# A decoder layer's stretch behind the head-pair loop: gating on GpSimd, the last two pairs projected in place, one half of the tokens ahead through both norms

## What is computed

```
x = x + attn(layernorm(x))        # a state-space scan
x = x + xattn(ctx, layernorm(x))  # 0.6 * sigmoid(si + sj + b) + 0.4 * layernorm(x)
x = x + moe(layernorm(x))
```

## Time and profile before

| | |
|---|---|
| median of three runs | 445.43 us (443.49 to 446.92) |
| the profiled execution | 447.58 us, span of its core 445.8 us |
| instructions | 8885 |
| PE busy | 414.9 us, 93% |
| DVE busy | 351.1 us, 79% |
| ACT busy | 225.7 us, 51% |
| POOL busy | 223.3 us, 50% |
| mean granted TensorE clock | 0.976 |

### The profile page before, as it was taken

How to read it: one execution, slowest core, us unless ns; L and a number is a source line. 1 busy time by engine, 2 the same in 40 slices (tenths; PEclk the granted TensorE clock), 3 DMA queues, 4 the chain that set the end, 5 groups by cost and what they waited for, 6 DMA issues and landing times.

```text
span 445.8 us, 8885 instructions
## 1 busy us (share of the span) xinstructions
PE 414.9 (93%) x2959; PEld 318.6 (71%) x2959; DVE 351.1 (79%) x604; ACT 225.7 (51%) x408; POOL 223.3 (50%) x238
## 2 busy tenths in 40 slices
PE   2898999999999999999999977998999999999995
PEld 1686767676667676667676556766789889899885
DVE  3787689889889889889889937947886696786775
ACT  5665545455545545545577430146543653554541
POOL 3444344654544664544577540022738558648661
PEclk9999799999999999999999978999899999999999
DMA  6302101221111212112210040011110201200002
GB/s 189 77 1 53 51 8 53 57 56 55 34 28 50 56 56 56 39 23 51 54 34 32 16 137 2 1 43 50 51 48 24 73 26 45 71 0 1 0 0 96
DMA packets 33607, 20.00 MB, mean 45 GB/s; under 512 B 15816, under 2 KB 31488, under 8 KB 33584
## 3 DMA queue, kind: packets, MB, share of 16 engines
q1 hardware_dynamic: 33584, 19.71, 15.7%
HBM read 17.33 MB, written 1.31 MB: 42 GB/s over the span
## 4 chain that ended last, share of the span: by engine, by line
PE 43%; issue 23%; POOL 14%; DVE 12%; ACT 3%; DMA 2%; SPq 1%; POOLq 1%; DVEq 0%; ACTq 0%
PE bank L1107 30%; POOL g L497 9%; PE bank L1131 4%; DVE conv L887 4%; POOL ce L490 3%; DMA w_raw<-in_L_attn_W_in_dram 1%; PE bank L1315 1%; DVE stats L814 1%; DMA ew_raw<-in_L_ffn_Wdown_dram 1%; ACT conv L561 1%; POOL xp L462 1%; PE bank L1475 1%; PE bank L1293 1%; DVE xres L1006 1%; SPq L325 1%
## 5 line engine op out<-in xcount | busy, mean ns | idle before, releaser
L887 DVE SCALAR_TENSOR_TENSOR conv<-bank,taps,conv 128x510 f32<-128x510 f32 (+2 forms) x204 | 151.6, 746 | 28.3 <-ACT conv L561 23.5
L497 POOL TENSOR_TENSOR g<-g,causal 128x512 f32<-128x512 f32 x64 | 81.6, 1294 | 108.1 <-DVE g L971 108.1
L1131 PE MATMUL bank<-uth,parts 128*128 128x512 f32 x272 | 98.6, 413 | 1.5 <-DVE utl L870 1.0
L561 ACT ACTIVATE conv<-bank,tap_b,taps 128x512 f32<-128x512 f32 x68 | 52.9, 779 | 77.2 <-PE bank L1131 76.8
L523 POOL TENSOR_TENSOR ul<-conv,uh 128x512 fp32r<-128x512 f32 x32 | 42.8, 1353 | 46.6 <-ACT uh L770 33.7
L528 POOL TENSOR_TENSOR parts<-conv,parts 128x512 fp32r<-128x512 f32 x30 | 44.2, 1502 | 36.0 <-ACT parts L784 35.9
L1131 PEld LDWEIGHTS bank<-uth,parts 128*128 128x128 f32 x272 | 51.8, 190 | 10.7 <-issue 1.7
L1131 PE MATMUL bank<-utl,parts 128*128 128x512 f32 x136 | 56.9, 418 | 0.0
L1107 PE MATMUL bank<-ewh,parts 128*128 128x256 f32 x256 | 46.2, 279 | 1.2 <-DVE parts L1094 1.2
L1079 DVE CAST uh<-conv 128x512 fp32r<-128x512 f32 x28 | 26.4, 977 | 22.7 <-ACT conv L766 22.4
L1315 PE MATMUL bank<-conv 64*128 64x128 f32 x512 | 43.4, 289 | 0.3 <-DVE conv L887 0.3
(11 more groups left out here) (204 smaller groups left out, 744.0 us busy)
## 6 DMA issues: line engine op xcount, KB each, us to landing
w_raw<-in_L_attn_W_in_dram SPq DMA_DIRECT2D x17, 256.0 KB, 3.2
ecx<-ecum_dram SPq DMA_DIRECT2D x32, 128.0 KB, 2.9
ew_raw<-in_L_ffn_Wup_dram SPq DMA_DIRECT2D x7, 256.0 KB, 2.8
ew_raw<-in_L_ffn_Wgate_dram SPq DMA_DIRECT2D x7, 256.0 KB, 3.1
ew_raw<-in_L_ffn_Wdown_dram SPq DMA_DIRECT2D x7, 256.0 KB, 3.8
xres<-in_x_dram SPq DMA_DIRECT2D x2, 512.0 KB, 4.1
out_dram<-xres SPq DMA_DIRECT2D x4, 256.0 KB, 2.3
yi<-yev SPq DMA_DIRECT2D x60, 16.0 KB, 1.9
```

The lines of the kernel that those rows point to most:

```text
L497: pool.tensor_tensor(g_v, g_v, causal[:].unsqueeze(1).to_broadcast([P, 4, P]), ALU.mult).then_inc(masked, 1)
L561: act.activation(conv[q][:, j, HALF * h:HALF * (h + 1)], bank[u % 2][:], ACT.Identity, bias=tap_b[q][:, j:j + 1], scale=taps[q][:, j, TAPS ...
L887: dve.scalar_tensor_tensor(out=dst[:, :, d:SEQ], in0=src[:, :, 0:SEQ - d], scalar=taps[q][:, j, TAPS - 1 - d:TAPS - d], in1=dst[:, :, d:SE ...
L1131: ins = pe.matmul(bank[u % 2][:], w, x_t, start=(i == 0), stop=(i == 3 * KD - 1))
```

## The change

- **Pairs.** Pairs 12 and 13 are written out as well. z's gate moves to pairs 12 and 13 (its scratch to `xn`), `pairwise` to pair 13, the scaling of `sig` to pair 14. `gate_y` moves from DVE to POOL: channel half 0 in pairs 13 and 14, half 1 in pair 15, there over its first 96 rows (`EARLY`, pairs 9 to 14).
- **Last two pairs.** Their y is not moved into `yi`. SP brings the matching rows of `zT`, `yD` and `woT` to where y lies (`load_late`, 24 DMAs in all). POOL gates pair 15's y in place (`gate_late`), DVE pair 16's, straight from PSUM (`gate_last`), and PE projects each 16 rows (`late_onto_o`). Every token tile has a bank of its own (`o_tile`).
- **Weights.** The loads of experts 0 and 1 go out in pairs 13 and 14; ACT splits expert 0's in pair 15, expert 1's at the end of the last; POOL makes the rests.
- **Norms.** Inverse roots start from ACT's square root with one Newton step. The first half of the tokens goes through both norms before the second half's first statistics. 58 of the matmuls that nothing reads go, 6 short ones come.
- **Expert 0.** Up starts on the first half, in banks 2 to 5. `route` takes the two-way softmax as `0.5 + 0.5 * tanh` of half the difference, and stands between products 1 and 2.
- **Down biases.** The probabilities are turned at expert 6; the biases are the first matmul of each tile's sum in the last `down`, and the `shift` goes into the last accumulation.

The diff, cut to its core and moved left by eight columns:

```diff
-    with eng.Fori(1, PAIRS // 2 - 1) as k:
+    with eng.Fori(1, PAIRS // 2 - 2) as k:
         body(2 * k, k, 0)
         body(2 * k + 1, k, 1)
-    for n in range(PAIRS - 2, PAIRS + 1):
+    for n in range(PAIRS - 4, PAIRS + 1):
         body(n, n // 2, n % 2)
 def last(n, ahead):
...
+def o_tile(t):
+    return bank[t][:, 0:DM]
+def up_bank(e, v):
+    return bank[2 + v] if isinstance(e, int) and e == 0 else bank[v]
...
+    def load_late(p):
+        r = slice(EARLY + 2 * HD * p, EARLY + 2 * HD * (p + 1))
+        for i in range(4):
+            rows_i = slice(32 * i, 32 * i + 2 * HD)
+            for a, src in enumerate((zT, yD)):
+                sp.dma_start(zsp[rows_i, p, a, :].rearrange("p (h t) -> p h t", h=2),
+                             src[r, 1, :].rearrange("p (h i t) -> p i h t", h=2, i=4)[:, i]).then_inc(zsp_in, 16)
+            sp.dma_start(wsp[rows_i, p, :], woT[r, 1, :]).then_inc(zsp_in, 16)
...
+        if n == PAIRS - 3:
+            load_expert(0, 0)
+        if n == PAIRS - 2:
+            sp.wait_ge(pair_read, 3)
+            load_expert(1, 1)
         if n < PAIRS:
             load_cum(n + 1, 1 - q)
-        if n > 1:
+        if 1 < n < PAIRS:
             sp.wait_ge(y_read, n - 1)
-            place_y(n - 1, 1 - q, (0, 1), yev_out[1 - q])
+            place_y(n - 1, 1 - q, yev_out[1 - q])
...
+        if n >= PAIRS - 1:
+            sp.wait_ge(z_gated, 4)
+            sp.wait_ge(y_init, 1)
+            sp.wait_ge(misc_read, 2)
+            load_late(n - PAIRS + 1)
...
+    def gate_y(k, half):
+        for q in range(2):
+            pool.wait_ge(yev_out[q], 64 * (PAIRS // 4 if k == 0 else PAIRS // 2 - 1))
+        r, c = slice(0, P if k == 0 else EARLY), slice(HALF * half, HALF * (half + 1))
+        link(pool.tensor_tensor(yi[r, k, c], yi[r, k, c], yD[r, k, c], ALU.add))
+        pool.tensor_tensor(yi[r, k, c], yi[r, k, c], zT[r, k, c], ALU.mult).then_inc(yz_done, 1)
+    def gate_late():
+        pool.wait_ge(y_read, PAIRS - 1)
+        pool.wait_ge(zsp_in, 24 * 16)
+        link(pool.tensor_tensor(yev[1][:], yev[1][:], zsp[:, 0, 1, :], ALU.add))
+        pool.tensor_tensor(yev[1][:], yev[1][:], zsp[:, 0, 0, :], ALU.mult).then_inc(late_gated[0], 1)
...
     def body(n, k, q):
+        end = isinstance(n, int) and n == PAIRS
+        if end:
+            decay_c_half(n, q, 0)
+            decay_c_half(n, q, 1)
         for u in range(4):
             pool.wait_ge(g_done, 4 * (n - 1) + u + 1)
             g_v = g[u % 2][:].rearrange("p (i k) -> p i k", k=P)
             pool.tensor_tensor(g_v, g_v, causal[:].unsqueeze(1).to_broadcast([P, 4, P]),
                                ALU.mult).then_inc(masked, 1)
-            if isinstance(n, int) and PAIRS - 2 <= n < PAIRS and 1 <= 4 * (n - PAIRS + 2) + u <= 4:
+            if isinstance(n, int) and PAIRS - 4 <= n < PAIRS - 2 and 1 <= 4 * (n - PAIRS + 4) + u <= 4:
                 v = (u - 1) % 4
                 pool.wait_ge(zgate_done, v + 1)
                 pool.tensor_tensor(z_part(v), z_part(v), zgate(v), ALU.mult).then_inc(z_gated, 1)
-            if u == 1:
+            if isinstance(n, int) and n in (PAIRS - 3, PAIRS - 2) and u == 3:
+                pool.wait_ge(z_gated, 4)
+                gate_y(0, n - PAIRS + 3)
+            if isinstance(n, int) and n == PAIRS - 2 and u == 2:
+                pool.wait_ge(sig_done, T)
+                pool.tensor_scalar(sig[:], sig[:], P_SEM / 2, P_SEM / 2, ALU.mult, ALU.add).then_inc(sig_scaled, 1)
+            if isinstance(n, int) and n == PAIRS - 1 and u >= 2:
+                gate_y(1, u - 2)
+            if u == 1 and end:
+                gate_late()
+            if u == 1 and not end:
                 decay_c(n, k, q)
                 if not last(n, 1):
                     at_least(pool, y_done, 4 * (n - 1))
                     prepare(n + 1, 1 - q)
-        if isinstance(n, int) and n == PAIRS:
-            pool.wait_ge(sig_done, T)
-            pool.tensor_scalar(sig[:], sig[:], P_SEM / 2, P_SEM / 2, ALU.mult, ALU.add).then_inc(sig_scaled, 1)
+        if end:
+            for e in range(2):
+                for j in range(3):
+                    rest_weights(e, e, j)
     over_pairs(pool, body)
...
         first_tap(m, km, r, u)
-        if isinstance(n, int) and n == PAIRS - 2:
+        if isinstance(n, int) and n == PAIRS - 4:
             gate_of_z(u)
-        if isinstance(n, int) and n == PAIRS - 1:
+        if isinstance(n, int) and n == PAIRS - 3:
             pairwise(u)
+        if isinstance(n, int) and n == PAIRS - 1 and u:
+            if u == 1:
+                act.wait_ge(ew_in[0], 48)
+            split_weights(0, 0, u - 1)
...
     def last_pair(n):
         decays(n, 0)
+        decays(n, 1)
+        evacuate_y(n - 1, PAIRS // 2 - 1, 1)
         copy_b(n)
-        evacuate_y(n - 1, PAIRS // 2 - 1, 1)
-        decays(n, 1)
-        act.wait_ge(ew_in[0], 48)
-        split_weights(0, 0, 0)
         copy_state(n)
         decays(n, 2)
         decays(n, 3)
-        evacuate_half(0)
-        split_weights(0, 0, 1)
-        split_weights(0, 0, 2)
-        evacuate_half(1)
+        act.preload_act_table(ACT.Sqrt)
+        act.wait_ge(ew_in[1], 48)
+        for j in range(3):
+            split_weights(1, 1, j)
...
     def expert(e, k, q):
         first = isinstance(e, int) and e == 0
+        if isinstance(e, int) and e == NE - 2:
+            for i in range(2):
+                act.wait_ge(prob_turned, i + 1)
+                act.copy(probT[:, HALF * i:HALF * (i + 1)], bank[4 + i][0:NE, :]).then_inc(prob_read, 1)
         act.wait_ge(eb_done, e + 1)
...
+            if first and v == 1:
+                root(slice(4, 8), 4)
             if first and v == 2:
+                copy_logits(0)
+                root(slice(T + 4, 2 * T), 5)
+                normalise(T + 4, range(4, 6), 5)
                 split_turned(6, 6)
                 split_turned(7, 7)
...
+            if first and v == 1:
+                act.wait_ge(pexp_in, 1)
+                act.activation(lg[:], lg[:], ACT.Tanh).then_inc(pexp_done, 1)
...
+    def inverse_roots(s, i, meanwhile=None):
+        dve.wait_ge(mv_done, i)
         dve.tensor_scalar(var[:, s], mv[:, s, 1], EPS, None, ALU.add)
-        dve.wait_ge(root_done, 1)
+        if meanwhile:
+            meanwhile()
+        dve.wait_ge(root_done, i)
         link(dve.reciprocal(rstd[:, s], rstd[:, s]))
...
+    def gate_last(h):
+        dve.wait_ge(y_done, 4 * (PAIRS - 1) + 2 * (h + 1))
+        if h == 0:
+            dve.wait_ge(yev_out[0], 64 * (PAIRS // 2 - 1))
+            dve.wait_ge(zsp_in, 24 * 16)
+        c = slice(P * h, P * (h + 1))
+        dve.tensor_tensor(yev[0][:, c], bank[7][:, c], zsp[:, 1, 1, c], ALU.add).then_inc(y_read, 1)
+        dve.wait_ge(y_read, PAIRS + h)
+        dve.tensor_tensor(yev[0][:, c], yev[0][:, c], zsp[:, 1, 0, c], ALU.mult).then_inc(late_gated[1], 1)
...
-                gate_y(0, 0)
-            if isinstance(n, int) and n == PAIRS:
-                if u == 1:
-                    gate_y(0, 1)
-                    split_router()
-                    rest_weights(0, 0, 0)
+                split_router()
         if isinstance(n, int) and n == PAIRS:
-            gate_y(1, 0)
+            gate_last(0)
...
-    moments(0, range(4), from_projection)
-    gate_y(1, 1)
-    inverse_roots(slice(0, 4))
     dve.wait_ge(sig_scaled, 1)
+    moments(0, range(4), from_projection, mv_done)
+    inverse_roots(slice(0, 4), 2, lambda: gate_last(1))
     second_block(range(4))
-    moments(T, range(4), from_residual)
-    moments(4, range(4, 8), from_projection)
-    inverse_roots(slice(4, 12))
-    normalise(10, range(2, 4))
+    moments(T, range(4), from_residual, mv_done)
+    inverse_roots(slice(T, T + 4), 3)
+    normalise(T + 2, range(2, 4))
+    rest_turned(4, 0)
+    rest_turned(5, 1)
+    moments(4, range(4, 8), from_projection, mv_done)
+    inverse_roots(slice(4, 8), 4)
     second_block(range(4, 8))
-    moments(12, range(4, 8), from_residual)
-    rest_turned(4, 4)
-    rest_turned(5, 5)
-    inverse_roots(slice(12, 16))
-    normalise(14, range(6, 8))
-    rest_weights(0, 0, 1)
+    moments(T + 4, range(4, 8), from_residual, mv_done)
+    inverse_roots(slice(T + 4, 2 * T), 5)
+    normalise(T + 6, range(6, 8))
     rest_turned(6, 6)
     rest_turned(7, 7)
...
-        link(dve.tensor_scalar(bg[:], sel[:], -NEG, NEG, ALU.mult, ALU.add))
+        link(dve.tensor_scalar(sel[:], sel[:], TOPK - 0.5, 0.5, ALU.is_lt, ALU.mult))
         link(dve.tensor_tensor(lg[:], lg[:], sel[:], ALU.mult))
-        link(dve.tensor_tensor(lg[:], lg[:], bg[:], ALU.add))
-        link(dve.tensor_reduce(mx[:], lg[:], AX.X, ALU.max))
-        dve.tensor_tensor(lg[:], lg[:], mx[:].unsqueeze(2).to_broadcast([P, T, NR]), ALU.subtract).then_inc(pexp_in, 1)
+        link(dve.tensor_reduce(mx[:], lg[:], AX.X, ALU.add))
+        dve.scalar_tensor_tensor(out=lg[:], in0=lg[:], scalar=2.0, in1=mx[:].unsqueeze(2).to_broadcast([P, T, NR]),
```

(91 more changed lines are left out.)

193 lines of the change are left out of this document (70 added, 123 removed).

## The result

The changed kernel takes 455.74 us (median of 4 runs, 454.62 to 456.43) against 445.31 for the kernel before (4 runs, 443.49 to 446.92): ratio 1.0215, 95% interval 1.0183 to 1.0247. It is slower by 10.4 us where 6.1 us less were forecast. The profiled execution took 456.43 us, with a span of 454.7.

A forecast was written before the change was run, and what follows sets the result against it. No engine bounds the whole span; 72.0 us between the last pair and expert 0's down product repeat nothing. Terms -10.8 + 3.7 + 1.0 = -6.1 from 445.43 gave 439.3 us; the range was 432 to 446.

The forecast's parts named there:

- Eight bias matmuls move into the last `down`, where nothing covers them: +3.7.: Last expert's down product: the bias matmuls moved there add 3.7 us uncovered.
- -10.8: Work from the last pairs to expert 0's down product: that product begins at 311.9 against 322.70, gaining 10.8 us.
- +1.0: Expert 6: the transposes of the probabilities stand in PE's queue and add 1.0 us.
- The rival for it: Clock falls more often, in up(0), second half and last `down`, as fillers go: together +4.1, 443.4 us; chance 0.15.
- down(0) at 311.9: Start of expert 0's down product, after the up(1) stall on silu 2 behind route: 311.9, against 322.70.
- First half: First half of tokens through projection and both norms: last rest ends at 277.0 against 289.3, gaining 12.3 us.
- ACT's 8.4 us wait: Last pair: ACT stands 8.4 us waiting for expert weights; its disappearance was a sign that the forecast holds.
- Late inputs: `gate_late` on POOL waits for 24 DMAs landing late: slower than before, up to +25 us, 464; chance 0.07.
- the 3 that I had named as a sign: POOL idle before `gate_late` for over 3 us would show the forecast wrong.
- The pairs did not stall: Rival that POOL's new gates and masks stretch and stall the pairs: +4.8 us, 444.1; chance 0.08.
- Second half and route: Second half's norms beside expert 0 end at 290.4; DVE starts `route` at 300.7, which takes 5.4 us, to 306.1.
- Three falls of the clock: Low clock after PE idles, about 1.7 us charged three times: first half's projection, up(0) and up(1).

The follow-up runs named there:

- experiment 2: Changed kernel with its biases as four grouped fp32 matmuls, 16 rows by 512 columns, ahead of the last down product: 446.17 us, ratio 1.0001.
- the kernel before with the tail part: Kernel before with only its expert 0 bias matmuls and their DVE additions replaced by eight 8-row fp32 ones in the last down product: 456.39 us.
- root and route: Changed kernel with f32r 128-row biases and filler, second half's first root ahead of up: 439.92 us; route ahead of DVE's products, no third filler: 439.03; both: 438.69.

## Why the prediction was wrong

*The step that failed: "Eight bias matmuls move into the last `down`, where nothing covers them: +3.7."* The product went from 5.7 to 20.6 us. By the rows: 3.5 for the matmuls (the product of 9.2 us over 128 rows); 2.4 for the eight changes of row count (8 x 0.3); the rest, 9.0, for half clock from the second tile to the end. Eight rows are the cause of the last two; 128 rows with zeros have neither. In the terms of the sum: +3.7 came out as +14.9, -10.8 as -7.4, +1.0 as +1.2. The rival for it, "the 8-row biases in the last `down` one more" fall, was priced at one fall among others, together +4.1. A fall after a group ends, as in experiment 2. With a few rows in every tile it does not: 19 us at half clock in a product that would have taken 9.

*What I overlooked stood in my own rows.* Of 315.46 to 322.70, clock 0.76, right behind the bias group of the kernel before, I said in the sum only that up(1) "ran partly at low clock too", and charged low clock there for idle PE alone, though PE was busy for all 7.2 us. The rival did tie the fall to the old bias block (with "0.5 to 0.75", where the row has 0.76): the row had been read, and left out of the forecast. I also took the pace of a bias from a group of sixteen pieces (3.71 us), which holds one change of row count and not eight.

*down(0) at 311.9.* It was at 315.33, 7.4 us earlier than before instead of 10.8. The kernel before without biases has it at 316.13. Its code is that of before up to the route, and its first half's last `utl` starts 1.2 us earlier (286.78 for 288.00); so 1.2 of the difference I put down to chance of the opening (the `ce` at 53.02 there and in the changed kernel, 54.43 in the profiled execution of before; granted clock 0.97 and 0.94 in the first 60 us), 5.4 is the bias group with the low clock behind it, and 0.8 is left for all that the change does behind the loop. The turns of prob take that back. In the 10.8 I had both kinds of gain in one number and never priced the group's removal by itself; it would have shown that everything else behind the loop was to bring 5.4.

*First half, nearly right.* Its last `utl` ended at 278.83 (277.0 forecast, 289.3 before), ACT's 8.4 us wait is gone, the masks of the last pair ended at 254.5 (256.0), the 24 DMAs had landed at 257.4 (259.5), `late_onto_o` took 1.15 us (1.5; the lower bound). Late inputs cost nothing: POOL stood 2.89 us for them, just under the 3 that I had named as a sign, while PE was still at the projection. The pairs did not stall. The 1.8 us of lateness are two operations of the root beside POOL's subtractions, 1.02 and 1.19 us where 0.2 each was charged.

*Second half and route, 4 late.* 294.4 for 290.4, and the route at 304.9 for 300.7: 1.8 from the first half, 0.6 more wait for the root than the 1.0 charged, 2.0 in the two operations stretched by POOL, which I had charged in the route alone. So the route began 4.5 us later than before. Three falls of the clock were charged, 5.0 us in all, and four came: at 252 to 254 (0.50), and 0.61, 0.56 and 0.52 in the table. The one at 0.61, over the turns of the first half, was charged nowhere. Taking the last three out gave 3.1 us.

*Experts.* Their period is 16.8 in the kernel before and the turns of prob cost 1.2 (17.97 for that expert; 1.0 forecast). In the kernels that start them early it is 17.0 to 17.2 for one to five of the experts and 17.2 to 17.9 for the first, where the waits that the profile names at PE's weight loads are for POOL's `ul` at the gate product; so part of any lead is spent there: the kernel before without biases is 6.6 us ahead at the first `down` and 4.2 at the last.

*The range and the chances.* 432 to 446 with 0.07 for slower: I named a clock under 0.9 in the last `down` as what would make it wrong, and gave it no price of its own. The -7.4 for -10.8 is no half hit either: 5.4 of it was the removal and 1.2 luck with the opening.

**Open.** How few rows, or how large a share of them, a product can hold before its clock falls: in the last product only 8 and 128 rows were run, 16 in a group, and 39 and 64 in the pairs, without a fall. Whether the few rows or the changes of row count bring it down. Why one run of the kernel before with the tail part took 449.2. What root and route are worth, each and together, since their intervals overlap and the traces show less than the medians.

## What to carry to other kernels

A matmul of 8 contraction rows inside a stream of full ones had two prices here that its columns don't show: the change of row count each way, and the clock. Pad it to 128 rows, zeros in one operand and finite numbers in the other, or leave it in one group where a low clock behind it costs nothing. When a low granted clock stands in a trace, look at the rows and kinds of matmul before it and not only at PE's idle time. Before you give a microsecond in a trace a meaning, find an early operation that both traces share and count from it. And price a removal by itself: here one small group that left a covered-looking place was nearly all of the gain of a rewrite.

## What the runs showed of the hardware that was not expected

- The granted clock stays at half for 19 us in which PE is busy 99.6% of the time (19.23 of 19.30), with 8-row matmuls between 128-row ones. The Trainium skill, "TensorE: Matmul & The Clock Gate", Part 1, has activity release the throttle; busy time as the profile counts it did not.
- The fall comes behind a group of few rows or over its end: in the kernel before, full clock over 3.5 us of 8-row matmuls, then 0.54 over the 3.7 us of 128-row ones that follow. With zeros up to 128 rows: 1.00.
- 16-row matmuls in four row groups, sixteen pieces in 1.15 us, 0.07 each; in one row group the 8-row ones take 0.23.
- 4-wide operations of DVE with two tiles as input, which take 0.16 us, took 1.04 and 1.27 beside two of POOL's 512-wide subtractions, and 1.02 and 1.19 in the first half.
